# A linear attention's gate made in the even iterations, and its denominators' guard made inside the products

## The reference

```python
def _L0_attn_ref(...):                      # one linear attention, 16 heads of 32
    v, p = jnp.split(_ln(x) @ W_in, 2, axis=-1)
    q, k = softmax(_ln(x) @ Wq + bq), softmax(_ln(x) @ Wk + bk)     # per head
    k = (1.0 - smear) * k + smear * k_prev
    q, k = q / s, k / s
    attn = jnp.tril(jnp.einsum('bhid,bhjd->bhij', q, k) * mask)     # decay in 8 heads, ones in 8
    norm = 1.0 / (attn.sum(axis=-1) + ATTN_EPS)
    o = jnp.einsum('bhij,bhjd->bhid', attn * norm[..., None], v)
    return _ln(jax.nn.silu(p) * o @ W_out)
def _L0_ffn_ref(...):                       # two layers
    ...                                     # local attention, 8 heads of 64, windows of 128
    h = a * jax.nn.gelu(g, approximate=False)
    x = x + h @ w2 + b2
```

## Time and profile before

| | us |
|---|---|
| median of 3 executions | 2001.72 (1994.23 to 2002.28) |
| the profiled execution | 1996.89 |
| its span, first to last instruction | 1995.1 |
| PE busy / weight loads busy | 1906.7 / 1635.3 |
| DVE busy | 1728.3 |
| ACT busy | 1196.3 |
| POOL busy | 1021.3 |

### The profile page before, as it was taken

The page is one execution under the profiler, slowest core; times in us unless marked ns, Lnnn a source line. Parts: engine busy times, 40 slices in busy tenths (PEclk is TensorE's granted clock), DMA queues, the critical chain, the costliest instruction groups (busy, mean ns, idle before and its releaser), DMA issues.

```text
span 1995.1 us, 48979 instructions
## 1 busy us (share of the span) xinstructions
PE 1906.7 (96%) x15178; PEld 1635.3 (82%) x15178; DVE 1728.3 (87%) x5308; ACT 1196.3 (60%) x2862; POOL 1021.3 (51%) x1004
## 2 busy tenths in 40 slices
PE   5899999999999999999999999999999999999998
PEld 3787888888888888888788888888888888888887
DVE  5888888988889888888877998888998888998886
ACT  3565655656556656566565665665665665666564
POOL 2554555645456554555534555545555545554542
PEclk8999999999999999999999999999999999999999
DMA  5010000000000100001102111111111101111101
GB/s 197 20 33 27 24 25 25 27 29 21 26 26 24 32 20 25 29 21 32 64 28 75 36 41 37 32 29 42 32 42 34 32 29 42 32 42 34 33 27 37
DMA packets 81152, 72.76 MB, mean 36 GB/s; under 512 B 13484, under 2 KB 74344, under 8 KB 81096
## 3 DMA queue, kind: packets, MB, share of 16 engines
q1 hardware_dynamic: 81096, 72.05, 11.8%
HBM read 42.64 MB, written 16.78 MB: 30 GB/s over the span
## 4 chain that ended last, share of the span: by engine, by line
PE 56%; DVE 20%; issue 14%; ACT 6%; POOL 2%; DVEq 1%; SPq 0%; POOLq 0%; ACTq 0%; DMA 0%
PE bank L1502 34%; PE bank L1507 11%; PE bank L1514 8%; PE bank L1549 3%; ACT L939 2%; DVE sq_sum L1294 2%; DVE prob L1041 2%; ACT gel L939 1%; DVE prob L1060 1%; DVE rot L1397 1%; DVE state L1093 1%; ACT mix_work L929 1%; DVE kT L1232 1%; DVE mix_work L1362 1%; DVE mix_work L1349 1%
## 5 line engine op out<-in xcount | busy, mean ns | idle before, releaser
L1502 PE MATMUL bank<-hT_n,w_s 128*128 128x128 f32 x3072 | 402.9, 281 | 22.9 <-ACT gel L939 22.0
L1502 PEld LDWEIGHTS bank<-hT_n,w_s 128*128 128x128 f32 x3072 | 364.7, 191 | 54.8 <-ACT gel L939 29.4
L823 ACT ACTIVATE prob<-prob,row_min 128x256 f32<-128x256 f32 x512 | 256.9, 505 | 168.1 <-DVE row_min L1041 167.7
L1507 PE MATMUL bank<-wqkv_s,xT 128*128 128x512 f32 x1152 | 320.1, 413 | 6.2 <-DVE wqkv_s L1214 3.4
L705 POOL TENSOR_TENSOR rot_other<-raw,rot_t 128x256 f32<-128x256 f32 x256 | 188.9, 769 | 221.8 <-ACT raw L792 221.8
L663 POOL TENSOR_TENSOR inv_norm<-sq_clip,half_neg 128x8 f32<-128x8 f32 x128 | 261.0, 2047 | 75.2 <-DVE sq_clip L1297 75.1
L1507 PEld LDWEIGHTS bank<-wqkv_s,xT 128*128 128x128 f32 x1152 | 208.2, 192 | 54.7 <-DVE wqkv_s L1214 5.4
L1041 DVE CUSTOM_DVE_ANT_0 prob<-bank,table,inv_norm 128x256 f32<-128x256 f32 x512 | 226.2, 478 | 3.4 <-issue 3.1
L1502 PE MATMUL bank<-w_s,hid 128*128 128x256 f32 x768 | 200.9, 385 | 0.0
L792 ACT ACTIVATE pT<-bank 128x512 f32<-128x512 f32 x256 | 140.2, 609 | 48.5 <-PE bank L1514 48.4
L1060 DVE TENSOR_SCALAR prob<-prob,row_inv 128x256 f32<-128x256 f32 x448 | 145.4, 367 | 8.0
(11 more groups left out here) (180 smaller groups left out, 4268.8 us busy)
## 6 DMA issues: line engine op xcount, KB each, us to landing
k_prev<-k_carry SPq DMA_DIRECT2D x32, 224.0 KB, 2.5
x_s<-in_L_attn_x SPq DMA_DIRECT2D x32, 128.0 KB, 2.1
rot_s<-in_rotary SPq DMA_DIRECT2D x64, 64.0 KB, 2.0
rows_normalised<-xh SPq DMA_DIRECT2D x32, 128.0 KB, 1.7
y_n<-rows_normalised SPq DMA_DIRECT2D x32, 128.0 KB, 2.2
x_between_layers<-x SPq DMA_DIRECT2D x32, 128.0 KB, 1.7
s_between_passes<-s_out SPq DMA_DIRECT2D x32, 128.0 KB, 1.7
x_s<-x_between_layers SPq DMA_DIRECT2D x32, 128.0 KB, 2.1
```

The lines of the kernel that those rows point to most:

```text
L823: ins = act.activation(prob[:, h, :], prob[:, h, :], ACT.Exp, bias=row_min[:, c:c + 1], scale=-1.0, accum_out=row_sum[:, c:c + 1])
L1502: return pe.matmul(out, lhsT, rhs, start=first, stop=last)
L1507: ins = pe.matmul(out, halved(left[:, a]), halved(right[:, b]), start=first and n == 0, stop=last and n == 2)
```

## The change

The product p moves from the odd iteration into the following even one: PE makes it ahead of `mix_out`, once the first two decayed scores have been read from the banks; DVE adds its bias into `gate`, ACT makes the tanh in `gate_tanh` (the memory of k_carry), POOL multiplies and adds. The gate is multiplied in one operation of 512 columns (`gate_read`) for two of 256.

The guard no longer has steps of its own. The column of ones in v_mix is now 2. For the eight heads without decay the guard stands in the state's column of sums, set up once. For the eight with decay PE gets two small products per chunk, q with four columns of `head_eps`. The reduction of q, `q_eps` and the denominators' sum are left out.

Moved besides: the weighing of a1 goes to ACT in odd iterations, the "sq" and "var2" steps and their root to the start of the window's own iteration; kT's low half ahead of xn; half of the state's additions behind xn; the first decayed scores behind the scores of a0; the last decayed scores behind xT's low half; u's v on PE ahead of the second part of the gate products.

```diff
@@ names
-        mix_pe = Steps(sem("mix_pe"), "q k v p kt qt s0 s1 s2 s3 o0 o1 gt wout")
+        mix_pe = Steps(sem("mix_pe"), "q k v kt qt s0 s1 s2 s3 p o0 o1 gt wout")
-        mix_act = Steps(sem("mix_act"), "xt tanh exp kt qt gt")
+        mix_act = Steps(sem("mix_act"), "xt exp kt qt tanh gt")
-            pool.memset(v_mix[:, :, MD:MV], 1.0).then_inc(setup_pool, 1)
+            pool.memset(v_mix[:, :, MD:MV], 2.0).then_inc(setup_pool, 1)
@@ POOL
+                if 1 <= i.low < NW:
+                    norm2(proj)
...
-                    pool.wait_ge(mix_act.sem, mix_act.at("tanh", n))
-                    pool.tensor_tensor(gate[:, :], p_tanh, p_lin, ALU.mult).then_inc(mix_pool.done("gatep"), 1)
...
+                if two is not None:
+                    pool.wait_ge(mix_act.sem, mix_act.at("tanh", two))
+                    pool.tensor_tensor(gate_tanh, gate_tanh, gate[:, :], ALU.mult).then_inc(mix_pool.done("gatep"), 1)
+                    pool.wait_ge(mix_pool.sem, mix_pool.at("gatep", two))
+                    pool.tensor_tensor(gate[:, :], gate_tanh, gate[:, :], ALU.add).then_inc(mix_pool.done("gate"), 1)
...
-                if i.low + 1 < NW:
-                    norm2(i.back(-1))
@@ ACT
                 if a is not None:
                     exps("a1", a)
                     exps("b0", a)
+                    if one is not None:
+                        weigh("a1", a)
...
+                if two is not None:
+                    act.wait_ge(mix_dve.sem, mix_dve.at("p", two))
+                    act.wait_ge(k_shifted, 48 * (two.number() + 1))
+                    act.activation(gate_tanh, gate[:, :], ACT.Tanh, scale=0.5).then_inc(mix_act.done("tanh"), 1)
                 if one is not None:
-                    act.wait_ge(mix_dve.sem, mix_dve.at("p", one))
-                    act.activation(p_tanh, p_lin, ACT.Tanh, scale=0.5).then_inc(mix_act.done("tanh"), 1)
@@ DVE, reading the products
-                dve.scalar_tensor_tensor(den, b[:, :, MD], 2.0, q_eps[:, g * MR:(g + 2) * MR],
-                                         ALU.mult, ALU.add).then_inc(mix_dve.done("den" + k), 1)
...
-                dve.reciprocal(rec, den).then_inc(mix_dve.done("rec" + k), 1)
+                dve.reciprocal(rec, b[:, :, MD]).then_inc(mix_dve.done("rec" + k), 1)
...
+            def gate_read(mix):
...
+                dve.wait_ge(mix_pool.sem, mix_pool.at("gate", mix))
+                dve.wait_ge(mix_dve.sem, mix_dve.at("o1", mix))
+                dve.tensor_tensor(go[:, :], go[:, :], gate[:, :], ALU.mult).then_inc(mix_dve.done("go"), 1)
@@ DVE, body
-                if two is not None:
-                    decay_scores(two, 0)
...
                 if two is not None:
+                    decay_scores(two, 0)
                     dve.wait_ge(mix_pool.sem, mix_pool.at("kdec", two))
                     decay_scores(two, 1)
...
                     weigh("a0", a)
+                if 1 <= i.low < NW:
+                    norm2_var(u)
+                if a is not None:
+                    if one is not None:
+                        inverse("a1", a)
...
+                if two is not None:
+                    dve.wait_ge(mix_pe.sem, mix_pe.at("p", two))
+                    dve.tensor_tensor(gate[:, :], mix_bank[1][:, :], bias_mix[:, 1, :], ALU.add)\
+                       .then_inc(mix_dve.done("p"), 1)
...
-                    dve.wait_ge(mix_pe.sem, mix_pe.at("p", one))
-                    dve.tensor_tensor(p_lin, mix_bank[1][:, :], bias_mix[:, 1, :], ALU.add)\
-                       .then_inc(mix_dve.done("p"), 1)
...
-                if one is not None:
-                    dve.tensor_reduce(qk_sum[:, 0:MH], heads(qk[:, 0:ME]), AX_X, ALU.add).then_inc(mix_dve.done("qsum"), 1)
...
-                    dve.tensor_tensor(q_eps[:, :], qk_sum[:, 0:MH], head_eps[:, :], ALU.mult)\
-                       .then_inc(mix_dve.done("qeps"), 1)
                 if two is not None and i.low < UNITS:
                     state_add(two, 0)
-                    state_add(two, 2)
...
+                if u is not None:
+                    low_turned(u, "kt", "kl", kT[:, :, :, u.parity, :], proj_bank)
                 if nxt is not None:
                     norm2(nxt)
-                if u is not None:
-                    low_turned(u, "kt", "kl", kT[:, :, :, u.parity, :], proj_bank)
+                if two is not None and i.low < UNITS:
+                    state_add(two, 2)
...
                     decay_scores(one, 2)
-                    decay_scores(one, 3)
                 if u_next is not None and one is not None:
                     low_turned_x(u_next)
+                if one is not None:
+                    decay_scores(one, 3)
@@ PE
                 mm(out, q_g, state[:, g, :], True, False)
+                if g < MG // 2:
+                    mm(out.rearrange("p (r c) -> p r c", c=MV)[:, :, MD], qT_mix[:, g, :],
+                       head_eps[:, g * MR:(g + 1) * MR], False, False)
...
                 if two is not None:
...
+                    pe.wait_ge(mix_dve.sem, mix_dve.at("s1", two))
+                    mix_linear(two, "p", mix_bank[1], win_s, ME)
...
-                if one is not None:
-                    pe.wait_ge(mix_dve.sem, mix_dve.at("k", one))
-                    mix_linear(one, "p", mix_bank[1], win_s, ME)
...
+                if u is not None:
+                    pe.wait_ge(proj_act.sem, proj_act.at("k", u))
+                    proj_linear(u, "v", 2 * E)
                 if m is not None:
                     pe.wait_ge(mlp_act.sem, mlp_act.at("g0", m))
                     hidden(m, mlp_bank[0], 0, HC + 4, 2)
-                if u is not None:
-                    pe.wait_ge(proj_act.sem, proj_act.at("k", u))
-                    proj_linear(u, "v", 2 * E)
```

More of the change, by code:

```diff
@@ L97, in constants @@
     masks = np.stack([own, before, own, none], 1)
+    own_rows = np.zeros((P, MG, MR), f)
+    for r in range(MR):
+        own_rows[r * MD:(r + 1) * MD, :, r] = 1
     parts = {
@@ L247, in build @@
         qk = mix_work[:, 0:2 * ME]
-        p_lin = mix_work[:, 2 * ME:3 * ME]
-        p_tanh = mix_work[:, 3 * ME:4 * ME]
         att = mix_work[:, :].rearrange("p (r g i) -> p r g i", r=MR, g=MG)
@@ L262, in build @@
         k_prev = sb("k_prev", [P, ME])
+        gate_tanh = k_carry[:, :]
         kT_mix = sb("kT_mix", [P, MG, P])
@@ L393, in build @@
         setup_dve = Steps(sem("setup_dve"), "rscale rneg rcopy q_0 kv_0 cols spread smear1 smear2 keep smear3 keep2 eps "
-                          "in_l mix_l bias half mlp_cols wo_0 q_1 kv_1 wo_1")
+                          "in_l mix_l bias half own eps_state mlp_cols wo_0 q_1 kv_1 wo_1")
         setup_pool = sem("setup_pool")
@@ L744, in body @@
                                        ALU.mult).then_inc(mix_pool.done("kdec"), 1)
+                if two is not None:
[3 more added lines that the diff above has]
+                    pool.tensor_tensor(gate[:, :], gate_tanh, gate[:, :], ALU.add).then_inc(mix_pool.done("gate"), 1)
+                if proj is not None and one is None:
+                    root(inv_norm[:, proj.parity, 0:H], sq_clip[:, 0:H], H).then_inc(proj_pool.done("invq"), 1)
                 if two is not None and i.low < UNITS:
@@ L1207, in halve_out @@
                 dve.wait_ge(table_loaded, 16)
+                dve.tensor_tensor(head_eps[:, :], head_eps[:, :], own_rows, ALU.mult).then_inc(setup_dve.done("own"), 1)
+                dve.wait_ge(setup_dve.sem, setup_dve.at("own", ONCE))
+                dve.tensor_copy(state[:, MG // 2:MG, :].rearrange("p g (r c) -> p g r c", c=MV)[:, :, :, MD],
+                                head_eps[:, MH // 2:MH].rearrange("p (g r) -> p g r", g=MG // 2))\
+                   .then_inc(setup_dve.done("eps_state"), 1)
                 dve.wait_ge(setup_pe.sem, setup_pe.at("mlp_cols", ONCE))
@@ L1342, in body @@
                        .then_inc(mix_dve.done("q"), 1)
-                if a is not None:
+                if two is not None:
+                    dve.wait_ge(mix_pe.sem, mix_pe.at("p", two))
+                    dve.tensor_tensor(gate[:, :], mix_bank[1][:, :], bias_mix[:, 1, :], ALU.add)\
+                       .then_inc(mix_dve.done("p"), 1)
+                if a is not None and one is not None:
+                    inverse("b0", a)
+                if a is not None and one is None:
                     weigh("a1", a)
-                    if one is not None:
-                        inverse("b0", a)
                 if one is not None:
@@ L1432, in body @@
                     low_out(a, 2, "pvb", "lb")
+                if two is not None:
+                    gate_read(two)
                 if m is not None and one is None and i.low != UNITS:
@@ L1729, in body @@
                 if two is not None:
+                    pe.wait_ge(mix_dve.sem, mix_dve.at("s1", two))
+                    mix_linear(two, "p", mix_bank[1], win_s, ME)
```

(3 more changed lines are left out.)

54 lines of the change are left out of this document (23 added, 31 removed).

## The result

The changed kernel takes **2079.68 us** (median of 4 runs, 2072.06 to 2091.08) against 1997.97 us for the kernel before (4 runs, 1992.53 to 2002.28). The ratio is 1.0405, with a 95% interval of 1.037 to 1.0441: slower by 4.1%. The forecast was 2015.6 us, between 1991 and 2029. The sign was right, and by luck: the loss comes from something of which the prediction doesn't speak, and without it, as the first experiment shows, the change makes no difference that counts. The profiled execution has a span of 2073.6 us at a mean granted clock of 0.976 (before: 1995.1 us, 0.993).

What follows compares the result with a forecast made beforehand. TensorE, busy 96% of the span, was taken as the bound. Terms 13.0 - 25.4 - 22.0 + 40.3 + 8.0 = +13.9 us on 2001.7 gave 2015.6 us, slower by 0.7%, range 1991 to 2029.

Steps and rivals of the forecast that it cites:

- small products: PE, even iterations: 64 four-column products at 0.20 us each, covered by nothing, +13.0 us.
- low half of kT, with what is left for xn: Layer 0: PE's waits for kT's low half go, as it moves ahead of xn; iteration 0's stays; -25.4 us.
- wait for GELU: PE's wait for ACT's GELU before the gate products' second part goes, with v put ahead as cover: -22.0 us.
- wait for kadd: Odd iterations: PE, rid of p, waits 1.26 us for DVE's kadd before k's transposes, 32 times, +40.3 us.
- two races: PE waits 0.1 us for hid in odd, 0.15 us for decayed scores in even iterations; 32 of each, +8.0 us.
- What costs nothing: DVE's changed steps, the gate's steps on POOL, and the tanh are covered by slack or other work: 0 us.
- The waits that go: PE's waits for kT's low half in layer 0 and for the GELU both go: -25.4 and -22.0 us.
- The race for hid: Odd iterations: w2's first part on PE needs hid, which follows kadd on DVE; 0.1 us late, 32 times.
- Rival 3: Even iterations: DVE falls behind because POOL's gate runs beside its longest steps; clearly slower, 2031 us, chance 0.13.
- Rival 2: a1's weighing doesn't delay the copy of k, or POOL's queue recovers it: about the same, 1997 us, chance 0.22.
- Rivals 1 and 4: First: kadd isn't last, faster, 1967 us, chance 0.10. Fourth: kT waits aren't shortened, xn now last, 2041 us, chance 0.03.

Runs made afterwards that it cites:

- the first experiment: The changed kernel with eight one-column memsets put ahead of VectorE's first instruction: 1993.79 us, ratio 0.9973 to the kernel before.
- after_dve8: The changed kernel with eight one-column memsets put ahead of VectorE's first instruction, nothing else changed: 1993.79 us, ratio 0.9973 to the kernel before.
- a1dve_qfirst: after_dve8 with a1's weighing back on VectorE and, in odd iterations, q turned before the smeared k on TensorE and evicted first by ScalarE: 1976.64 us, ratio 0.9902.
- after_dve1: The changed kernel with one memset put ahead of VectorE's first instruction: 2075.85 us in one run.
- after_dve90: The changed kernel with 90 memsets put ahead of VectorE's first instruction: 1995.29 us, ratio 0.9981.
- before_dve100: The kernel before with 100 one-column memsets put ahead of VectorE's first instruction: 2065.71 us, ratio 1.0333.

## Why the prediction was right and wrong

Compared are the profiled executions of before (span 1995.1 us) and of after_dve8 (1994.5), which is the change without the stops. The difference is -0.6 us; the runs' medians say -0.3%. The forecast's sum was +13.9. (It was put on a median of 2001.7 us for the kernel before; with more runs that median is 1997.5 to 1998.6.)

| term | forecast, us | measured, us | from |
|---|---|---|---|
| small products | +13.0 | +14.1 | busy time of TensorE, with and without them |
| low half of kT, with what is left for xn | -25.4 | -24.8 | 28.8 gone, 4.0 for xn |
| wait for GELU | -22.0 | -21.3 | 0.7 left, in one place |
| wait for kadd | +40.3 | +28.3 | 34.4, less the 6.1 that before has in two places outside the steady turns (row below) |
| two races | +8.0 | +4.9 | neither came; a wait for pT did |
| sum | +13.9 | +1.2 | span: -0.6; the set-up's wait for wqkv_s is 1.9 shorter |
| VectorE's code fetched in each turn | not there | +79.1 | after against after_dve8 |

```profile
PE bank L1514 <- DVE mix_work L1415: 6.1, 2, 3.8
```

**The step that failed** is a term that stood at nothing. "What costs nothing" and the rest of the sum price every instruction by its own duration and by the work that hides it, and let the number of instructions cost nothing. It cost 79.1 us. Two smaller terms were sized wrongly, the wait for kadd (12.0 us too large) and the two races (8.0 us, and neither came). Without the stops the time of 1993.8 us would have lain in the range, at its low end, but not on the side of slower that was forecast.

**The small products** were read rightly from the row of the same operand shape. The 0.20 us are 0.22. In the time line of after, group by group, they stand as the rows of 33 columns stood in the earlier trace rows:

```profile
744.07 0.39 PE L1521 MATMUL bank<-state,qT_dec 128*128 128x132 f32 x2
744.30 0.28 PE L1521 MATMUL bank<-head_eps,qT_mix 128*128 128x4 f32 x2
744.44 1.06 PE L1521 MATMUL bank<-v_mix,mix_work 128*128 128x33 f32 x8
```

Two records start at 744.30 and the next ones at 744.44. By their starts the first pair takes less than the forecast's 0.20 here; what the products cost in all is told by leaving them out. The lower bound of 8.7 us, and the estimate of 3 us from the Trainium skill's floor of a small matmul ("TensorE: Matmul & The Clock Gate"), are both ruled out. The same page's rule on weight loads (LDWEIGHTS; 0.107 us for 128 columns) gives an estimate of 13.7 us for the 128 records, and the measured 14.1 agree.

**The waits that go** were right to within 1 us, and so was the reason: PE had nothing else to wait for there.

**The wait for kadd** was right in cause and place and 12 us too large. In the steady turns it is 0.70 us in layer 0 and 1.07 in layer 1; the forecast was 1.26 for both, with 0.1 more for layer 0. By the table of the chain above two things were off. The copy of k to raw is put off by 0.29 and 0.49 us and not by 0.58, most clearly in layer 0, so that layer 0 is not the worse one. And TensorE asks 0.3 to 0.5 us later than forecast. Some 0.16 us of that is the way of counting: the forecast counted distances of starts, by which the loss is 0.87 and 1.23 us, while the profile's idle time begins at a matmul's modelled end. Some is the wait for pT, which the sum didn't have. In layer 1 one thing goes the other way: the first product of rot on VectorE takes 1.98 us in place of the 1.65 of the earlier trace rows, and kadd comes that much later.

**The races** didn't come: PE's table of after has 0.8 us for the decayed scores in all, and no row for hid. The race for hid became real, at 16.8 us, when PE no longer waited for kadd (a1dve_qfirst). The wait for pT, 4.9 us in 27 places, was in no part of the sum.

**Iterations.** In layer 1 a turn of the loop is 1.08 us longer (59.45 to 60.53), where the forecast had +1.2. In layer 0 it is 1.19 shorter (61.46 to 60.27), where it had -0.5.

**The rivals.** Rival 3, that VectorE would fall behind because POOL makes the gate beside its long steps, didn't come. By the view of groups the k norm's mean went from 1178 to 694 ns, that of rot's first product from 1410 to 1628, that of its sum from 1246 to 1344, and these three groups together became shorter (245.3 to 234.6 us). A fourth became longer by more than that, here before and in after_dve8:

```profile
L1297 DVE TENSOR_SCALAR sq_clip<-sq_sum 128x16 f32<-128x16 f32 x64 | 28.6, 447 | 2.2
L1316 DVE TENSOR_SCALAR sq_clip<-sq_sum 128x16 f32<-128x16 f32 x64 | 55.2, 862 | 2.2
```

So VectorE's slow steps changed their place and didn't go away. That POOL's work beside them is what stretches them was not tested by itself. What VectorE stood still for in the even iterations was its code. Rival 2 (1997 us) describes after_dve8's time well, and not by its own reason: the weighing does delay the copy. Rivals 1 and 4 didn't come.

**What was missing** is a term that no row of an instruction carries. The number of instructions had a price of its own: 15 fewer ahead of a loop moved its head across an edge. The page of before shows the other state of it, 25 packets on the instruction queue and none while the loops run, and nobody asks of a quiet row what would wake it. Had the prediction looked at the queue, it could have named the rival; where the edge is, the trace of before alone would have told only roughly.

That position sets the stops is shown: after, after_dve1, after_dve8 and after_dve90 differ in the number of memsets alone, as do before and before_dve100. That the loop is lost because four pieces and the one fetched ahead are more than are kept is a reading: three touched pieces stayed in every run (before, after with 8 and with 90, and the six other variants, whose loops begin 6 to 14 instructions above an edge by the same count and whose pages have 25 or 26 packets on q14), four never did (after, after with 1, before with 100), and in each such turn five packets came. What happens with a loop of four pieces under another way of fetching wasn't tried. The Trainium skill ("Advanced Engine Details and Errata", ISA Cache) gives 32 KB of code for an engine other than TensorE, in two lines of 16 KB. By the reading above the traces here agree with the total (three pieces and one ahead are kept) and not with the lines: q14's packets are 8,192 bytes, and the edges lie 134 and 125 records apart. With lines of 256 a turn of 278 records would meet two edges at most; here it met three, near its 4th, 138th and 263rd record.

## What to carry to other kernels

When a change adds or removes instructions on an engine whose code doesn't fit at once, look at the instruction queue in the profile of both kernels: packets in a steady loop mean that its code is fetched again, and "issue" at the head of the loop is where it shows. Before judging such a change, shift the code by a few empty instructions; here that moved the result from 4.1% slower to 0.3% faster, which is no difference that counts. And when a wait on the engine that bounds the kernel is filled, work out the next step in its own queue before counting the gain: the fill here paid 4.5 us by itself, and another 17 once the step behind it was reordered too.

## What the runs showed that was not expected

- A loop of 278 executed records on VectorE ran 7.0 us per turn longer (67.28 against 60.27) when it began two instructions below an edge of its code, with two stops of about 2.0 and 2.4 us, one for each of two packets of 8,192 bytes.
- A stop of 2.6 us per turn cost nearly as much as one of 4.5 (71.1 and 79.1 us of span), since the granted clock stayed at 0.5 for about 10 us behind eight of the twelve; more of the loss was slower work (41.5 us) than waiting (29.4).
- A product of four columns against a stationary operand of 128 cost 0.22 us as a pair of f32 records. The 38 us of steps on VectorE that the products save were free where they lay.
